# Transformer block on one core: x for V's last tiles in four transfers, the first residual eight halves later, Q/K weights asked for ahead of stores, Q/K pieces respaced

## What is computed

```python
xq, xk, xv = x @ wq.T, x @ wk.T, x @ wv.T           # 16 heads of 32
probs = softmax(einsum('bqhd,bkhd->bhqk', xq, xk))  # over k, float32
x = layernorm(x + einsum('bhqk,bkhd->bqhd', probs, xv) @ wo.T)
p = softmax(x @ Wr.T + br)
e, weight = argmax(p), max(p)
y = einsum('nd,erd->ner', x, A)                     # 8 x 64
y = einsum('ner,eor->neo', y, B) / 64
out = layernorm(x + y[token, e] * weight)
```

## Time and profile before

| | |
|---|---|
| median of 3 runs | 1531.58 us (1528.26 to 1532.74) |
| the profiled execution | 1529.98 us, of which the core's span is 1528.1 us |
| PE busy | 1457.9 us, 95% of the span |
| POOL, DVE, ACT busy | 1143.6, 977.8, 785.9 us |
| mean granted PE clock | 0.98 of 2.4 GHz |
| chain that ended last | 84% of it on PE, 7% DVE, 3% DMA |

### The profile page before, as it was taken

The page is one execution under the profiler, slowest core; times in us unless marked ns, Lnnn a source line. Parts: engine busy times, 40 slices in busy tenths (PEclk is TensorE's granted clock), DMA queues, the critical chain, the costliest instruction groups (busy, mean ns, idle before and its releaser), DMA issues.

```text
span 1528.1 us, 21319 instructions
## 1 busy us (share of the span) xinstructions
PE 1457.9 (95%) x7176; PEld 911.8 (60%) x7176; DVE 977.8 (64%) x1850; ACT 785.9 (51%) x1430; POOL 1143.6 (75%) x651
## 2 busy tenths in 40 slices
PE   7999999999899999999999899999999999999997
PEld 5755556666545666666555566666655566565376
DVE  6747666665465676665566567666546677775674
ACT  3445655655454555555455455545544556555332
POOL 0367879888687779877679778889767899999411
PEclk9999999999899999999999999999999999999999
DMA  7345636563633434356353434234544122220001
GB/s 228 103 129 151 220 105 200 160 220 86 214 98 107 124 96 118 98 146 201 96 168 105 139 108 141 57 112 138 165 127 152 29 50 64 50 64 22 22 1 56
DMA packets 85628, 178.36 MB, mean 117 GB/s; under 512 B 19584, under 2 KB 26768, under 8 KB 84368
## 3 DMA queue, kind: packets, MB, share of 16 engines
q1 hardware_dynamic: 70240, 133.46, 30.4%
q10 hardware_dynamic: 14944, 42.47, 7.9%
q0 software_dynamic: 336, 1.07, 0.3%
HBM read 119.30 MB, written 56.88 MB: 115 GB/s over the span
## 4 chain that ended last, share of the span: by engine, by line
PE 84%; DVE 7%; issue 3%; DMA 3%; ACT 1%; POOL 1%; SPq 1%; ACTq 0%; POOLq 0%; DVEq 0%
PE w L695 25%; PE pv L854 15%; PE sc L842 14%; PE mx L832 14%; PE w L739 6%; DVE mxc L1153 3%; PE mx L806 3%; PE mx L695 1%; PE mx L766 1%; PE w L747 1%; PE sc L695 1%; DMA den_parts<-spread_s 1%; DMA stack<-mrow 1%; DMA wqk_s<-wqk_parts 1%; PE mx L755 1%
## 5 line engine op out<-in xcount | busy, mean ns | idle before, releaser
L1153 DVE TENSOR_REDUCE mxc<-mx 128x1 f32<-128x512 f32 x1024 | 682.7, 686 | 423.2 <-PE mx L832 420.0
L998 ACT ACTIVATE P<-sc 128x512 f32<-128x512 f32 x1024 | 603.3, 598 | 504.7 <-PE sc L842 482.0
L594 POOL TENSOR_TENSOR Psum<-Psum,P 128x1024 f32<-128x1024 f32 x286 | 674.1, 2384 | 24.3 <-ACT P L998 22.6
L842 PE MATMUL sc<-stack 98*128 98x512 f32 x1024 | 463.6, 455 | 10.0 <-DMA stack<-mrow 6.5
L832 PE MATMUL mx<-stack 96*128 96x512 f32 x1024 | 409.7, 405 | 11.1 <-DVE eq L1292 4.3
L842 PEld LDWEIGHTS sc<-stack 98*128 98x128 f32 x1024 | 194.6, 190 | 100.4 <-issue 36.7
L854 PE MATMUL pv<-P,V 128*32 128x512 f32 x2048 | 253.0, 613 | 0.0
L832 PEld LDWEIGHTS mx<-stack 96*128 96x128 f32 x1024 | 196.1, 192 | 90.6 <-issue 28.4
L591 POOL TENSOR_TENSOR Psum<-P 128x1024 f32<-128x1024 f32 x50 | 118.8, 2392 | 136.0 <-ACT P L998 103.9
L695 PE MATMUL w<-xT_s,wqk_s 128*128 128x512 f32 x504 | 163.2, 415 | 14.4 <-DVE xT_s L1169 10.5
L854 PEld LDWEIGHTS pv<-P,V 128*32 128x32 f32 x2048 | 56.7, 111 | 132.9 <-issue 106.9
(11 more groups left out here) (172 smaller groups left out, 1273.5 us busy)
## 6 DMA issues: line engine op xcount, KB each, us to landing
stack<-qk_parts SPq DMA_DIRECT2D x186, 256.0 KB, 4.3
qk_parts<-split SPq DMA_DIRECT2D x56, 512.0 KB, 3.5
wqk_s<-wqk_parts SPq DMA_DIRECT2D x40, 512.0 KB, 4.4
den_s<-den_parts SPq DMA_DIRECT2D x124, 64.0 KB, 2.0
r_f<-x ACTq DMA_DIRECT2D x3, 2048.0 KB, 12.9
wide<-a_parts ACTq DMA_DIRECT2D x3, 2048.0 KB, 8.2
out<-r_f SPq DMA_DIRECT2D x12, 512.0 KB, 3.4
xT_s_f<-xT ACTq DMA_DIRECT2D x5, 1024.0 KB, 8.0
```

Source lines behind the costliest of these rows:

```text
L594: pool.tensor_tensor(sums(s)[:, i, :], sums(s)[:, i, :], P[:, unit % NP, :], ALU.add).then_inc(add_done, 1)
L842: pe.matmul(sc[c][:, :], stack(s, i)[0:KS, 0, 128 * kb:128 * kb + 128], stack(s, i)[0:KS, 1, 512 * c:512 * c + 512], start=True, stop=True ...
L998: act.activation(P[:, unit % NP, 512 * c:512 * c + 512], sc[c][:, :], ACT.Exp).then_inc(exp_done, 1)
L1153: dve.tensor_reduce(mxc[:, q % 2, at:at + 1], BANK["max", g][:, :], AX.X, ALU.max).then_inc(mx_done, 1)
```

## The change

Four edits, in two tables, in SP's order and in ACT's order.

1. `again_x` takes a quarter t: 128 of the 512 tokens, 512 KB, in rows of 512 bytes (before: one transfer of 2 MB). The four are issued at half 29 of slot 15 (23) and halves 2, 5 and 8 of slot 16 (24), with a semaphore each, and V tile 4+t waits for its own.
2. `load_res` of batch 0 is issued at half 20 of slot 8 instead of 12.
3. SP issues `load_weights` one half after the end of the piece that frees the place, before that half's stores; before it stood behind the piece's own store, two halves after its end.
4. The entries of `some` two to four go from (2, 0), (1, 1), (1, 0) to (1, 1), (1, 0), (1, 1), and the piece list has room for a `qk` between the first `h` and the second `t1`.

```diff
-        some = [(1, 1), (2, 0), (1, 1), (1, 0), (1, 0), (0, 0), (1, 0), (1, 1), (1, 1), (1, 0)] if fill else [(0, 0)] * (KB + 2)
+        some = [(1, 1), (1, 1), (1, 0), (1, 1), (1, 0), (0, 0), (1, 0), (1, 1), (1, 1), (1, 0)] if fill else [(0, 0)] * (KB + 2)
...
-        pieces = take(0, 0) + [("t1", at)] + take(0, 1) + [("lg", at)] + take(1, 0) + [("h", at), ("t1", at + 1)]
+        pieces = take(0, 0) + [("t1", at)] + take(0, 1) + [("lg", at)] + take(1, 0) + [("h", at)] + take(1, 1) + [("t1", at + 1)]
...
-            AGAIN_X[HALVES * PAIRS * batch - 7] = batch
+            for t in range(KB // 2):
+                AGAIN_X[HALVES * PAIRS * batch + (-3, 2, 5, 8)[t]] = batch, t
...
+                for n in ends(half - 1, "qk"):
+                    if n >= 16 and n == last_of(load_of(n)) and load_of(n) + 2 < LOADS:
+                        load_weights(load_of(n) + 2)
                 for n in ends(half - 2, "qk"):
                     store_qk(n)
-                    if n >= 16 and n == last_of(load_of(n)) and load_of(n) + 2 < LOADS:
-                        load_weights(load_of(n) + 2)
...
-                        pe.wait_ge(x_again, 16 * (b - 1))
+                        pe.wait_ge(x_again[kb % 4], 16 * (b - 1))
...
-                act.dma_start(xT_s[:, :, :, :].bitcast(f32), x_d[b - 2]).then_inc(x_again, 16)
+                at = slice(128 * t, 128 * t + 128)
+                act.dma_start(xT_s[:, :, :, at].bitcast(f32), x_d[b - 2][:, :, :, at]).then_inc(x_again[t], 16)
...
-                if h == 12 and p == 0 and b:
+                if h == (20 if b == 1 else 12) and p == 0 and b:
                     load_res(b - 1)
```

More of the change, by code:

```diff
@@ L338, in build_attention_lora_moe_block @@
         a_loaded, b_loaded = sem("a_loaded"), sem("b_loaded")
-        x_kept, x_again = sem("x_kept"), sem("x_again")
+        x_kept, x_again = sem("x_kept"), [sem(f"x_again{t}") for t in range(KB // 2)]
         yT_hi, hmT_hi = sem("yT_hi"), sem("hmT_hi")
@@ L925, in keep_x, with again_x @@
                 act.dma_start(x_d[b - 2, :, :, kt, :], xT_s[:, :, kt, :].bitcast(f32)).then_inc(x_kept, 16)
-            def again_x(b):
+            def again_x(b, t):
                 act.wait_ge(qk_ready, 16 * (b + 1))
                 act.wait_ge(v_ready, KB * b + KB // 2)
-                act.dma_start(xT_s[:, :, :, :].bitcast(f32), x_d[b - 2]).then_inc(x_again, 16)
+                at = slice(128 * t, 128 * t + 128)
+                act.dma_start(xT_s[:, :, :, at].bitcast(f32), x_d[b - 2][:, :, :, at]).then_inc(x_again[t], 16)
             def load_raw_ab(n):
@@ L1094, in _ @@
                 if half in AGAIN_X:
-                    again_x(AGAIN_X[half])
+                    again_x(*AGAIN_X[half])
                 for n, place in enumerate(SPLIT_AT.values()):
```

## The result

| | before | after |
|---|---|---|
| median | 1532.16 us (4 runs, 1528.26 to 1533.68) | 1505.03 us (4 runs, 1502.79 to 1506.54) |
| ratio | | 0.9826, 95% interval 0.9802 to 0.9849 |
| profiled execution, span | 1529.98, 1528.1 us | 1506.31, 1504.5 us |
| mean granted PE clock | 0.981 | 0.993 |

The kernel is 27.1 us faster by the medians and 23.7 us by the profiled executions; 26.9 was forecast. Lines have moved by two or three (806 is now 808, 842 is 844).

What follows compares the result with a forecast made beforehand. PE was taken to bound the kernel through its work, its waits and the clock lowered behind them. Terms of 9.3, 11.3, 6.5 and -0.2 us sum to 26.9, giving 1505 us, range 1499 to 1518 us.

Steps and rivals of the forecast that it cites:

- Part 1: Start of slot 9: with the residual later, PE's wait for POOL's last add falls from 7.25 to 0.55 us; 9.3 us.
- the quiet slot: One slot before slot 8, without the residual's transfer: the next step followed the reciprocals' store after 4.5 us.
- Part 2: Slots 15 and 23: x in four transfers behind the row maxima removes most of PE's waits for them; 11.3 us with clock.
- Part 3: Both PE waits for Q/K weights and their clock go, less 0.8 us for the delayed store; 6.5 us.
- the shorter weights wait: PE's wait of 1.4 us for Q/K weights, forecast to go because the request also leaves the stack's 768 KB behind.
- Part 4: Respaced pieces: two waits for `hm` (1.7 us) go, 1.9 us of waits for `eq` come; -0.2 us.
- The two new waits: PE's waits for `eq` at `lg` 0 and `lg` 2 after the respacing, 1.3 and 0.6 us.
- The maxima of slot 9: Rival: the later residual delays slot 9's row maxima; 3.3 us of wait and 2.6 of clock return, 1511 us; chance 0.16.
- ACT's stand for x in slot 9: ACT would stand 2 us for batch 2's x in slot 9; nothing taken off for PE, 2 us as bound.
- Waits in the second row: Rival: small waits of SP, ACT and POOL take the place, 1.5 us in each of seven places; 1515 us, chance 0.16.
- The long wait: Rival: the change doesn't reach PE's wait at slot 9's start, POOL itself setting slot 8's end; 1514 or 1525 us, chance 0.07.
- The 512-byte rows: Rival: x pieces can't keep up, V tile 7 waits 28 us in both batches; slower, 1534 us, chance 0.03.

Runs made afterwards that it cites:

- the repeat: The changed kernel run once more with nothing altered: 1504.38 us, ratio 0.9847.
- two pieces behind: The changed kernel, but for the last two Q/K pieces of a batch the weights are again asked for behind the store: 1504.86 us, ratio 0.9833.
- the runs of parts 4 and 1: The kernel before with only the respaced Q/K pieces: 1525.01 us; and with only the first residual moved to half 20 of slot 8: 1523.95 us.

## Why the prediction was right, step by step

The total was right: 1505.0 forecast, 1505.03 measured. That the two meet within 0.03 us is luck. One kernel's executions lie 4 to 8 us apart, and errors of the terms offset each other: parts 1 and 3 gave less than their sums, and 1.5 us came in a slot that no part names. The terms, by slot lengths, and by the repeat for slots 8 and 9, where after's own profile had the longest wait of all:

| part | forecast | measured, us |
|---|---|---|
| 1 residual | 9.3 | slots 8 and 9: 8.4 in the repeat, 6.1 in after |
| 2 x pieces | 11.3 | slots 15, 16, 23, 24: 10.7 ("two pieces behind", so that part 3 is out of it) |
| 3 weights | 6.5 | slots 10 and 17: 4.2; slot 15: -1.8; 2.4 |
| 3 or 4 | | slot 18: 1.9, which either part alone also gave |
| 4 respacing | -0.2 | slot 11: -0.9; slot 19: 0.5; -0.4 |
| sum | 26.9 | 23.0, and slot 25: 1.5 |

Slot 25 has the same work and waits; before, the clock fell in it, and in after and the repeat it didn't, so it is no term of a part that I can name. 24.5 us in the slots against 26.9 forecast: the sum was a little high. The medians give 27.1 for reasons outside the sum: the repeat reached slot 8 1.5 us earlier than before, and before's profiled execution lies 2.2 us under its median, where the forecast had put 1.6.

**Part 1.** The store of the reciprocals landed in 4.7 us, 4.5 had been forecast, and the residual itself took 8.4 us. The step that failed is the one behind: "the next step followed the store after 4.5 us" was all that the sum took from the quiet slot, and the loads behind the store were taken to be as there. SP and POOL in slot 8 of after:

```profile
383.06 0.43 SPq L507 DMA_DIRECT2D den_parts<-spread_s  x1
387.73 3.16 SPq L512 DMA_DIRECT2D den_s<-den_parts  x4
```

```profile
392.56 2.66 POOL L630 TENSOR_TENSOR attT_f<-pv_s,den_s 64x512 f32<-64x512 f32 x2 [3.00 <-issue]
395.29 16.43 POOL L596 TENSOR_TENSOR Psum<-Psum,P 128x1024 f32<-128x1024 f32 x7
```

The four loads took 3.16 us to issue, and 2.4 to 3.1 in the nine other profiled executions with a later residual, where the quiet slot and slot 8 of before had 1.71, and POOL stood 3.00 us. It ended 1.97 us after PE instead of 0.55 (1.40 in the repeat), and the clock fell, as it did in none of the other nine. So two of the forecast's signs, a wait under 1 us and a full clock, failed in after. The residual has no hand in that, since a still later one left 1.90 us. Why the issue takes longer here than in slot 16 (1.84 us in after) stays open.

**Part 2.** As forecast: 0.3 us for the maxima where 0.5 was allowed, full clock, no wait for a piece (they landed in 4.5 us in the median, 6.8 at most, where 4 was forecast, and the first V tile wanted its own 9.6 us after its issue). What the forecast did not see is how narrow the margin is: it put the first piece "behind" the maxima, and by the traces it leaves 0.1 us after the fourth. The issue cost ACT 0.53 to 0.60 us a piece, not 0.4. The lower bound of 7 us for this part was also added up wrongly: 11.3 less 1.7 us of clock twice is 7.9.

**Part 3.** The waits and the clock went as forecast. Two steps failed. The store's price was put at 0.8 us and was 1.8, in slot 15, and not because the store travels behind 512 KB: SP stood for the weights with the spread of the sums and the store behind it. With the weights ahead as the only change slots 15 and 16 took 3.4 us more than before, though 0.9 and 1.3 of such a difference stand in the runs of parts 4 and 1 too, which leave these slots alone. And the sum took for granted that PE keeps what it gains, but in slots 10 and 18 POOL's work sets the end: the shorter weights wait with its clock, 3.1 us in the forecast, gave 1.1 in slot 10.

**Part 4.** The two new waits came where they were expected, 0.83 us (1.3 forecast) and 0.82 us (0.6 forecast), and the two for `hm` went. In slot 10 none of it counts, for POOL's sake. In slot 18 it does, and together with the clock it made up for slot 11.

**The rivals.** The maxima of slot 9 weren't delayed, and ACT's stand for x in slot 9 was nothing in after and 1.29 us in the repeat (2 forecast). Waits in the second row did take places, but three and not seven: 1.05, 1.69 and 2.23 us, the last of which costs nothing against a PE with a lower clock. The long wait was reached. The 512-byte rows kept up; that rival's time was added up wrongly as well, since waits of 56 us on top of 1505 give 1561 us and not 1534.

## What to carry to other kernels

Before adding up what waits are worth, look at each stage for the engine that works through it without a gap: here POOL's 35.45 us in a slot of 37.1 capped what two parts gained in it, and in before it was busy 35.46 us of the same slot, which then took 39.1. A request that its engine must wait for holds up everything behind it in that engine's order, so look at what stands there before moving it forward. A transfer that is issued "behind" an urgent one on another queue is only behind it if its margin is larger than the urgent one's issue time. And compare stage lengths between traces before trusting a difference of medians under 0.5%.

## What the runs showed of the hardware

- Small transfers on one queue waited for a large one that was issued first on another: up to 3.3 us behind 2 MB in rows of 16 KB in before, 2.6 us in one slot and 0.4 in the other behind 2 MB in rows of 512 bytes. They did not always wait for all of it: one moved after more than half of 2 MB (66 rows of 16 KB and some more).
- A lead of 0.3 us in issue decided whether the last of four small transfers moved before 2 MB or in the midst of it: no wait, or 5.57 us.
- An issue of 1024 rows of 512 bytes took ACT 0.53 to 0.60 us alone and 1.2 us each where four followed one another (4.93 us); one of 2 MB in large rows took 0.34 us. Four loads of 64 KB took SP from 1.71 to 3.16 us to issue, for a reason that the runs don't show.
- The same wait of 0.85 us at the same place was followed by a clock of 0.79 over 8 us in one execution and 1.00 in another; after 1.97 us it fell, after 1.90 us it didn't. So a wait didn't fix what the clock did behind it, and executions of one and the same kernel lay up to 7.6 us apart (1503.46 and 1511.06).
